# A spiking attention block with a mixture of experts: the last chunk norms from row sums and ScalarE squares, and new orders at both ends

## The reference

```python
def lif_step(v, x_t):              # a leaky neuron: halve the gap, spike at 1, reset
    v = v + (x_t - v) * 0.5
    s = spike(v - 1.0)
    v = v * (1.0 - s)
    return (v, s)

def step(carry, inp):              # scan over the 512 steps
    vr, r = lif_step(vr, r_in); vk, k = lif_step(vk, k_in); vv, v = lif_step(vv, v_in)
    h = h * 0.9 + k * v
    y = r * h

x1 = layernorm(x + y @ Wo.T, ln1_g, ln1_b)          # norm 0
s1 = lif_scan(x1 @ W1.T + b1)
ffn = lif_scan(s1 @ W2.T + b2)
a = layernorm(x1 + ffn, ln2_g, ln2_b)               # norm 1
x3 = _layernorm(x + a)                              # norm 2, the "third" of the title
gates = softmax(x3 @ Wg + bg); keep the best 2 of 8, rescaled
out = _layernorm(x3 + sum over e of gate_e * (x3 @ We_e + be_e))   # norm 3, the "last"
```

## Time and profile before

| | us |
|---|---|
| median of 3 runs | 991.33 (990.92 to 992.54) |
| the profiled execution, its own time | 988.63 |
| its span, first to last instruction | 986.8 |
| PE, DVE busy in the span | 925.7 (94%), 915.6 (93%) |
| ACT, POOL busy in the span | 611.8 (62%), 571.8 (58%) |

### The profile page before, as it was taken

The page is one execution under the profiler, slowest core; times in us unless marked ns, Lnnn a source line. Parts: engine busy times, 40 slices in busy tenths (PEclk is TensorE's granted clock), DMA queues, the critical chain, the costliest instruction groups (busy, mean ns, idle before and its releaser), DMA issues.

```text
span 986.8 us, 20602 instructions
## 1 busy us (share of the span) xinstructions
PE 925.7 (94%) x6506; PEld 859.1 (87%) x6506; DVE 915.6 (93%) x3682; ACT 611.8 (62%) x1389; POOL 571.8 (58%) x731
## 2 busy tenths in 40 slices
PE   5678789999999999999999999999999999999985
PEld 5578688999999999999999999999999999888764
DVE  6489998999999999999999999999999999988975
ACT  4565546666666676666666766667667666556452
POOL 1221113667676666666766666677766666765552
PEclk8799999999999999999999999999999999999999
DMA  8552222555554456555554555655545665456763
GB/s 259 129 108 66 42 54 55 118 119 118 108 112 107 100 122 119 119 122 107 114 107 99 119 118 120 127 111 104 113 97 114 119 127 110 97 97 118 141 127 86
DMA packets 59437, 109.71 MB, mean 111 GB/s; under 512 B 6592, under 2 KB 6592, under 8 KB 59328
## 3 DMA queue, kind: packets, MB, share of 16 engines
q0 software_dynamic: 37728, 68.71, 40.6%
q1 hardware_dynamic: 16992, 31.30, 9.7%
q10 hardware_dynamic: 4608, 8.39, 2.2%
HBM read 31.29 MB, written 8.39 MB: 40 GB/s over the span
## 4 chain that ended last, share of the span: by engine, by line
PE 73%; DVE 15%; ACT 3%; issue 3%; DMA 3%; POOL 2%; SPq 0%; POOLq 0%; ACTq 0%; DVEq 0%
PE ps_e L401 28%; PE ps_proj L401 12%; PE ps_proj L491 10%; PE ps_proj L476 10%; PE ps_proj L497 5%; PE ps_attn L401 3%; DVE U L887 3%; DVE V L894 2%; PE ps_zx L455 2%; DVE stats L966 2%; PE ps_attn L455 1%; DVE h L936 1%; DMA xt<-x_hi 1%; DMA xt<-x_T 1%; DMA acc<-term 1%
## 5 line engine op out<-in xcount | busy, mean ns | idle before, releaser
L887 DVE SCALAR_TENSOR_TENSOR U<-V,U 128x256 f32<-128x256 f32 (+4 forms) x576 | 227.7, 395 | 6.6 <-ACT U L658 2.9
L401 PE MATMUL ps_e<-we_hi,x_hi 128*128 128x512 f32 (+2 forms) x640 | 228.6, 357 | 3.6 <-DVE acc L1109 1.9
L894 DVE SCALAR_TENSOR_TENSOR V<-U 128x256 f32<-128x256 f32 (+4 forms) x576 | 224.2, 389 | 1.6
L401 PE MATMUL ps_e<-we_lo,x_hi 128*128 128x512 f32 (+2 forms) x640 | 223.3, 349 | 0.0
L401 PE MATMUL ps_e<-we_hi,x_lo 128*128 128x512 f32 (+2 forms) x640 | 222.7, 348 | 0.0
L1331 POOL TENSOR_SCALAR s<-U 128x256 fp32r<-128x256 f32 x208 | 192.1, 971 | 16.3 <-DVE V L894 16.3
L1317 POOL TENSOR_SCALAR veps<-mv 128x2 f32<-128x2 f32 x128 | 50.6, 396 | 256.6 <-DVE mv L972 254.4
L697 ACT ACTIVATE term<-ps_e,gate 128x256 f32<-128x256 f32 x372 | 160.3, 475 | 43.3 <-PE ps_e L401 43.3
L658 ACT ACTIVATE U<-ps_proj,cst 128x256 f32<-128x256 f32 x320 | 135.4, 480 | 70.5 <-PE ps_proj L497 64.1
L491 PE MATMUL ps_proj<-x_hi,w_hi 128*128 128x256 f32 x512 | 134.9, 284 | 3.1 <-ACT x_hi L676 1.7
L643 ACT ACTIVATE U<-ps_proj 128x512 f32<-128x512 f32 x96 | 57.6, 600 | 127.2 <-PE ps_proj L401 127.2
(11 more groups left out here) (108 smaller groups left out, 2302.3 us busy)
## 6 DMA issues: line engine op xcount, KB each, us to landing
acc<-term POOLq DMA_DIRECT2D x93, 256.0 KB, 3.7
odd_sum<-term POOLq DMA_DIRECT2D x93, 256.0 KB, 3.3
xt<-x_T SPq DMA_DIRECT2D x33, 256.0 KB, 2.9
xa<-x_tok SPq DMA_DIRECT2D x32, 256.0 KB, 3.2
xt<-x_hi POOLq DMA_DIRECT2D x32, 256.0 KB, 4.3
xb<-cst SPq DMA_DIRECT2D x32, 256.0 KB, 2.3
xb<-x_tok POOLq DMA_DIRECT2D x32, 256.0 KB, 6.1
out<-res ACTq DMA_DIRECT2D x31, 256.0 KB, 2.0
```

What stands on the lines that cost most here:

```text
L401: mm = pe.matmul(dst, lhs, rhs, start=(i == 0), stop=(i == n - 1))
L887: v.scalar_tensor_tensor(out=U[:, s, t, c0:c1], in0=V[:, c0:c1], scalar=0.5, in1=U[:, s, t, c0:c1], op0=ALU.mult, op1=ALU.add).then_inc(do ...
L894: v.scalar_tensor_tensor(out=V[:, c0:c1], in0=u, scalar=THRESHOLD, in1=u, op0=ALU.is_lt, op1=ALU.mult).then_inc(done, 1)
```

## The change

It does the following.

- Norms 2 and 3 no longer use bn_stats and bn_aggr. The VectorE instruction that makes the row also gives its sum (`accum_out`). POOL turns the sums into the negated mean; ScalarE runs two `Square` activations with that mean as bias and accumulates the squares; POOL makes the variance and the power; VectorE multiplies. `res` of norm 3 is made by two instructions of 256 columns instead of one of 512.
- In a steady beat the two squares of norm 2 stand after the first W1 eviction, those of norm 3 after the fourth.
- The x of the second chunk is loaded ahead of the constants and Wo. Its low part is made by VectorE in beat 0, slot 2, not by the POOL DMA and `low_x`.
- TensorE runs 14 further matmuls, whose result nobody reads, after the first R/K/V product (`bridge`).
- In beats 1 to 6 several slots move: norm 0's shift from 8 to 7, the gates, `add_e0`, x1_low (19 in beats 3 and 4, 15 in beat 6), norm 2's shift from 16 to 15, x3_low from 25 to 28. `norm_x3` goes behind the W2 eviction.
- In beats 33 to 38 slots move, the e0 product of the next beat goes ahead of expert step 6, and POOL serves norms 1 and 2 ahead of two of its DMAs.

```diff
-            gate=(4, 5, 6, 7, 8, 12, 13, 14, 15, 16, 24, 26), add_e0=(17, 18),
-            ln1_sum=1, ln1_stats=(2, 3), ln1_aggr=4, ln1_norm=8, x1_low=17,
+            gate=(4, 5, 6, 7, 8, 10, 10, 11, 11, 12, 24, 26), add_e0=(13, 14),
+            ln1_sum=1, ln1_stats=(2, 3), ln1_aggr=4, ln1_norm=7, x1_low=17,
...
-            ln3_stats=10, ln3_aggr=11, ln3_shift=16, x3_low=25,
+            ln3_stats=10, ln3_aggr=11, ln3_shift=15, x3_low=28,
...
+X1_LOW = {3: 19, 4: 19, 6: 15}
+DRAIN = dict(z_sum=-1, y=(-1,) * 5, spikes_h1=-1, fin_sum=11,
...
-             fin_add=17, fin_stats=18, fin_aggr=19, fin_shift=27)
+             fin_add=25, fin_stats=26, fin_aggr=27, fin_shift=31)
+TAIL = dict(DRAIN, add_e0=(5, 5), ln2_scale=(3, 4), x3_low=17)
...
             def beat(b):
-                if b.has(LAG_X):
+                if b.has(LAG_X) and b.k != LAG_X + 1:
                     load_xt(b)
...
                 if b.k == LAG_X:
+                    load_xt(Beat(LAG_X + 1))
                     sp.dma_start(cst[:], consts).then_inc(consts_loaded, 16)
                     sp.dma_start(wo[:], w_o).then_inc(wo_loaded, 16)
...
+            def bridge():
+
+                for _ in range(BRIDGE):
+                    pe.matmul(ps_attn[:, 0, :], wrkv_hi[:, 0, 0:P], wrkv_hi[:, 0, 0:D], start=True, stop=True)
...
+                        if part == 6 and b.late and not b.last_m:
+                            expert0(Beat(b.k + 1))
                         expert(b, part)
                         if part == 4 and b.has(LAG_Z) and b.late:
                             x3_T(b)
-                    if b.late and not b.last_m:
-                        expert0(Beat(b.k + 1))
...
+            def square(ln, src, junk):
+
+                for j in range(TILES):
+                    last = nc.scalar.activation(junk[:, j, :], src[:, j, :], ACT.Square, bias=minus_mean[ln][:, j:j + 1],
+                                                accum_out=squares[ln][:, j:j + 1])
+                last.then_inc(squares_ready[ln], 1)
+
+            def square_x3(b):
+                act.wait_ge(mean_ready[2], b.value(1, LAG_Z, 1))
+
+                if b.has(LAG_Y):
+                    act.wait_ge(x1T_done, b.value(1, LAG_Y, 1))
+                square(2, w, x1n)
+
+            def square_res(b):
+                act.wait_ge(mean_ready[3], b.value(1, LAG_F, 1))
+                square(3, res_of(b), odd_sum[:, b.slot(LAG_F, 2)])
...
                     for f in (0, 1):
                         to_lif(b, fill + f, COL_H1 + 2 * f * B, 2, C_B1 + 2 * f)
+                        if f == 0 and b.has(LAG_Z) and not b.early:
+                            square_x3(b)
...
                     to_lif(b, fill + 3, COL_H1 + 6 * B, 2, C_B1 + 6)
+                if b.has(LAG_F) and not b.late:
+                    square_res(b)
...
                 v.scalar_tensor_tensor(out=w[:, j, :], in0=w[:, j, :], scalar=rstd[1][:, j:j + 1],
-                                       in1=xb[:, j, :], op0=ALU.mult, op1=ALU.add).then_inc(ln2_steps, 1)
+                                       in1=xb[:, j, :], op0=ALU.mult, op1=ALU.add,
+                                       accum_out=sums[2][:, j:j + 1]).then_inc(ln2_steps, 1)
...
-                    v.tensor_tensor(res[:], acc[:, b.slot(LAG_F, 2)], odd_sum[:, b.slot(LAG_F, 2)],
-                                    ALU.add).then_inc(fin_steps, 1)
...
+                    total(odd_sum[:, b.slot(LAG_F, 2)])
...
+            def x_low_second():
+                dve.wait_ge(x_hi_ready, 2)
+                v.scalar_tensor_tensor(out=x_lo[:], in0=xt[:, 1], scalar=-1.0, in1=x_hi[:].bitcast(F32),
+                                       op0=ALU.mult, op1=ALU.subtract).then_inc(x_lo_ready, 1)
...
+            def deviation(b, ln, steps, per, lag, done):
+
+                pool.wait_ge(steps, b.value(per, lag, done))
+                g.tensor_scalar(minus_mean[ln][:], sums[ln][:], -1.0 / D, None, ALU.mult).then_inc(mean_ready[ln], 1)
+                pool.wait_ge(squares_ready[ln], b.value(1, lag, 1))
+                g.tensor_scalar(veps[ln][:], squares[ln][:], 1.0 / D, EPS, ALU.mult, ALU.add).then_inc(rstd_ready[ln], 1)
+                pool.wait_ge(rstd_ready[ln], b.value(2, lag, 1))
+                g.tensor_tensor(rstd[ln][:], veps[ln][:], neg_half[:], ALU.pow).then_inc(rstd_ready[ln], 1)
...
+                if has_z and b.late:
+                    reciprocal_std(b, 1, ln2_steps, LN2_STEPS, LAG_Z, 4)
                 if sums:
                     add_even(b, LAG_F, 6)
```

More of the change, by code:

```diff
@@ L80 @@
 WARM = 5
+BRIDGE = 14
 TERM_SLOTS = E - 2
@@ L246, in build @@
         gate_T = sb("gate_T", [STACK, TILES, P], F32R)
-        stats = [sb(f"stats{i}", [P, TILES, 6]) for i in range(4)]
-        mv = [sb(f"mv{i}", [P, TILES, 2]) for i in range(4)]
+        stats = [sb(f"stats{i}", [P, TILES, 6]) for i in range(2)]
+        mv = [sb(f"mv{i}", [P, TILES, 2]) for i in range(2)]
+        sums, minus_mean, squares = ({i: sb(f"{name}{i}", [P, TILES]) for i in (2, 3)} for name in ("sums", "minus_mean", "squares"))
         veps = [sb(f"veps{i}", [P, TILES]) for i in range(4)]
@@ L285, in build @@
         rstd_ready = [sem(f"rstd_ready{i}") for i in range(4)]
+        mean_ready, squares_ready = ({i: sem(f"{name}{i}") for i in (2, 3)} for name in ("mean_ready", "squares_ready"))
         e0_done, expert_done = sem("e0_done"), sem("expert_done")
@@ L801, in beat @@
                     fill += 1
+                if b.has(LAG_Z) and b.early:
+                    norm_x3(b)
                 if b.has(LAG_Y) and not b.early:
@@ L817, in beat @@
                     read_x3(b)
+                if b.has(LAG_Z) and b.late:
+                    square_x3(b)
                 if b.has(LAG_M) and not b.early and not b.last_m:
@@ L850, in beat @@
                         weight_high(p)
-                if b.has(LAG_X) and b.k > LAG_X:
+                if b.has(LAG_X) and b.k > LAG_X + 1:
                     low_x(b)
@@ L857, in beat @@
                             read_x3(b)
+                        if part == 5 and b.has(LAG_F) and b.late:
+                            square_res(b)
+                if b.has(LAG_F) and (b.last_m or b.k == LAST_BEAT):
+                    square_res(b)
                 if b.has(LAG_F):
@@ L1116, in fin_stage, with total @@
             def fin_stage(b, step):
-                chain = lambda n: after(fin_steps, FIN_STEPS, LAG_F, b, n)
                 if step == 0 and b.k == LAST_BEAT:
                     return
+                def total(other):
+                    for j in range(TILES):
+                        v.scalar_tensor_tensor(out=res_of(b)[:, j, :], in0=acc[:, b.slot(LAG_F, 2), j, :], scalar=1.0,
+                                               in1=other[:, j, :], op0=ALU.mult, op1=ALU.add,
+                                               accum_out=sums[3][:, j:j + 1]).then_inc(fin_steps, 1 + (j == 0 and b.k == LAST_BEAT))
                 if step == 1 and b.k == LAST_BEAT:
@@ L1122, in fin_stage @@
                     dve.wait_ge(term_ready, b.value(E - 1, LAG_F, E - 1))
-                    v.tensor_tensor(res_of(b)[:], acc[:, b.slot(LAG_F, 2)], bias_bank(b.k - 1)[:], ALU.add).then_inc(fin_steps, 2)
+                    total(bias_bank(b.k - 1))
                     return
@@ L1167, in side @@
                 split_w1(b, slot)
+                if b.k == 0 and slot == 2:
+                    x_low_second()
                 if b.k == LAG_Y + 1 and slot == 2 * STEPS - 1:
@@ L1213, in side @@
                             gate_stage(b, step)
-                if b.has(LAG_Y) and slot == at["x1_low"]:
+                if b.has(LAG_Y) and slot == X1_LOW.get(b.k, at["x1_low"]):
                     x1_low(b)
@@ L1227, in side @@
                         ln2_add(b, 1)
-                    if slot == at["ln3_stats"]:
-                        after(ln2_steps, LN2_STEPS, LAG_Z, b, 8)
-                        bn_stats(2, 0, w[:, 0, :], ln3_steps)
-                        bn_stats(2, 1, w[:, 1, :], ln3_steps)
-                    if slot == at["ln3_aggr"]:
-                        bn_aggr(b, 2, ln3_steps, LN3_STEPS, LAG_Z, 2)
                 if b.has(LAG_M):
```

34 lines of the change are left out of this document (16 added, 18 removed).

## The result

The changed kernel takes 1014.01 us, the median of 4 runs (1011.92 to 1014.18), beside 991.31 for the kernel before on the same chip (990.92 to 992.54): a ratio of 1.0222, 95% interval 1.0204 to 1.0240. Forecast were 1009 and a range of 981 to 1023. The profiled execution has a span of 1010.1 us against 986.8, 23.3 more.

The account below looks back on a forecast made before the run. PE bounds the kernel, without a gap in steady beats of 28.06 us. 27.3 (steady) - 7.7 (start and fill) - 1.6 (drain) = +18.0 on 988.63 gives 1006.6; the median lies 2.7 above, so 1009, range 981 to 1023.

Parts of the forecast that it names:

- The steady beats: Beats 7 to 32: two pairs of squares on ACT make PE late, 26 x 1.05 = +27.3 us.
- The stretch on ACT: Steady beat, first W1 eviction to expert step 4's: 7.61 us, 0.96 of it waits; both pairs of squares go there.
- p: Time one pair of squares holds ACT in a steady beat: taken as 1.0 us, by norm 2's pair at 0.99.
- The second ring: Steady beats: squares and POOL make norm 3's shift on DVE 1.5 us later; 0.05 us a beat, 0 to 0.3.
- rival 4: Steady beats: DVE becomes the bound through waits at slots 24 and 29; beat 29.5, time 1018; chance 0.13.
- The start: Second chunk's x loaded earlier: PE's second product at 14.4, third from 27.1 to 29, its end about 5.9 us earlier.
- Beats 3 to 6: Moved slots: beat 3 -0.3, beat 5 +0.4, beat 6 -0.55 and -1.4; together -1.85 us.
- The drain: Last beats: earlier reciprocal and e0 product against slower norms; sum -1.6 us, from -7 to +3.
- reciprocal ahead: Drain, beat 36: POOL's reciprocal of norm 1 ahead of accumulating DMAs is done about 2.3 us earlier, -2.3.
- e0 ahead: Drain: e0 product ahead of step 6 brings the next beat's gates 1.4 us earlier; two beats counted, -2.8.
- longer norm chains: Drain: norms 2 and 3 pass more engines, 0.7 us for each of five norms on the chain, +3.5.
- rival 3: Steady beats: the accumulator read is dear, 1.2 to 1.4 us a pair of squares; time 1024; chance 0.12.

Follow-up runs that it names:

- squares_ahead: Changed kernel with norm 2's scale and add two slots earlier and its squares ahead of the first W1 eviction in steady beats: 1021.88 us, ratio 1.0293.
- edges_only: Changed kernel with norms 2 and 3 by bn_stats and bn_aggr as before, all new orders of start, fill and drain kept: 982.7 us.
- old_drain: edges_only with the whole drain as in the kernel before (slots, POOL's order, e0 product behind expert step 6): ratio 0.9886 to the kernel before.
- pool_only: no_bridge with the changed kernel's drain order on POOL alone, norms by bn_stats: 983.69 us, ratio 0.9916 to the kernel before.
- no_e0_ahead: edges_only with the e0 product of the next beat again behind expert step 6 in the drain: ratio 0.9905 to the kernel before.
- norms_pool: Kernel before with norms 2 and 3 by squares, norm_x3 behind the W2 eviction, and the changed kernel's drain order on POOL alone: 1020.90 us, ratio 1.0286.
- warm_gap: old_drain with 45 more unused matmuls ahead of the first attention product: 979.48 us, ratio 0.987 to the kernel before.
- no_bridge: old_drain without the 14 bridging matmuls ahead of the second product: 979.61 us, ratio 0.9874 to the kernel before.

## Why the prediction was right, and where it was off

**The steady beats: right, step by step.** The stretch on ACT is closed, the pair is 0.98 (I took 1.0), PE waits for `term` before step 6. It waits before step 5 too, which I had not named: 0.27 and 0.74 in the beat shown, and 19.7 / 21 = 0.94 a beat over all. Gates of beat 6 to 32 give +26.0 against +27.3. The beat is 0.96 longer than the one before counted alike (28.10; my 28.06 came from a window that was not 21 whole beats), and I had 1.05. The row that I chose for p, norm 2's pair, was the right one of two: a pair of squares with their sums takes 0.98, that pair 0.99. By the Trainium skill, ScalarE: Activation LUTs, section Rules for kernel authors, the estimate was 1.04 a beat, and the trace agrees to 0.1.

**The second ring.** I put 0.05 on it and made it rival 4 at 0.13. It did not decide, but `squares_ahead` bears out that it was close, 0.17 us a beat by the count of DVE's waits, and waits of 0.89 and 1.74 at the two shifts (forecast about 1 and 1.5) filled it. The sum of rival 4 does not come out: 2.5 us of waits less 0.65 of slack and 1.4 of saved work is 0.45, a beat of 28.5 and not 29.5. Measured, DVE's work fell by 1.1 only, and 26.29 of work and 2.61 of waits are 28.90 of the 29.06. That the ring stayed behind the queue was close, and partly luck.

**The start: right.** PE's second product starts at 13.81 (forecast 14.4), the attention product runs at half clock as bounded, the third product starts at 27.92 (27.1 to 29). Rows of the changed kernel that answer to the earlier trace rows:

```profile
13.81 0.39 PE L407 MATMUL ps_proj<-x_hi,wrkv_hi 128*128 128x256 f32 x1 [0.71 <-DVE x_lo L1204]
```
```profile
24.73 3.75 PE L444 MATMUL ps_attn<-wo,wrkv_raw 128*128 128x256 f32 x8 [6.41 <-DVE wrkv_raw L1002]
27.92 0.78 PE L407 MATMUL ps_proj<-x_hi,wrkv_hi 128*128 128x256 f32 x1
```

**Beats 3 to 6: the sign right, the size too small.** In beat 5, which the earlier trace rows show before, norm 2's shift waits 1.33, not 2.2, and `x3_low` no longer waits. In beat 6 PE's wait for an eviction is gone, and its wait for norm 0 falls from 3.45 to 2.06. What the prediction said of `x1_low` in beat 5 came true: it stands behind the shift, and PE waits 1.60 for it (at 121.14). The slots and the place of `norm_x3` are worth 4.6 us with norms off. What the squares take back in the fill is not shown: `edges_only` and the changed kernel have -11.5 and -10.0 by the gates of beat 6, but `old_drain`, with the same fill code as `edges_only`, has -8.1. That spread is in the profiles, where the granted clock is at 0.50 in other places, and I can't price it.

**The drain: the step that failed.** I had -1.6, as -2.3 (reciprocal ahead), -2.8 (e0 ahead) and +3.5 (longer norm chains); it is +7.3. The chains are near: 7.3 - 4.4 = 2.9 between the changed kernel and `edges_only`, from one profile each. Both gains were not there, though the reciprocal of the earlier trace rows did come ahead and DVE's wait for it fell from 1.25 to 0.38. I had followed the waiting instruction forward to its own consumer and had not asked what stood behind it in the queue that it passed. The e0 product passed step 6, and ACT's `gexp` stood behind step 6. The reciprocal passed a DMA, and the sum of the outputs, in its old slot, stood behind that DMA (`pool_only`). The changed kernel has the sum in a later slot and is spared that wait; but I had not priced the new place of norm 3 at all: its sum now stands behind `x3_low`, and its shift (slot 31) directly ahead of the next `z`. DVE and PE of the changed kernel, beat 34 to 35:

```profile
946.32 0.69 DVE L1063 TENSOR_TENSOR x_lo<-ps_zx,x_hi 128x512 fp32r<-128x512 f32 x1 [1.44 <-ACT x_hi L656]
...
947.25 0.42 DVE L1169 SCALAR_TENSOR_TENSOR res<-acc,odd_sum 128x256 f32<-128x256 f32 x1
...
950.58 0.16 DVE L1021 TENSOR_TENSOR shift<-minus_mean,rstd 128x2 f32<-128x2 f32 x1 [1.31 <-POOL rstd L1365]
950.69 0.76 DVE L954 SCALAR_TENSOR_TENSOR z<-U,x 128x256 f32<-128x256 f32 x2
```
```profile
951.50 0.66 PE L461 MATMUL ps_zx<-cst,z 128*128 128x128 f32 x4 [1.07 <-DVE z L954]
```

3.3 us from the sum to the shift, 1.31 of them waited out, and PE idles 1.07 for `z`. Before, the sum of this beat ran 2.5 us ahead of `x3_low` (927.59 against 930.05) and the shift found its input ready. In `edges_only`, which has the slots without squares, beats 34 to 35 take 17.04 against 15.80; with squares 18.27. `no_e0_ahead` has 17.05, so it is not the e0 order. `norms_pool`, with the old slots and only POOL's order new, loses +4.7 in its drain instead of +7.3, from one profile each.

So of the new orders only POOL's belongs to the squares: in the old slots it gains 13 us with them and loses 4 with `bn_stats`. The new slots and the e0 order lose with `bn_stats` (3.4 by the ratios, POOL's order included), and with squares the drain that has them is 2.6 longer than that of `norms_pool`; by the ratios the gap is no smaller. Which of the two makes it with squares was not run apart. Taken one by one against the kernel before, as I took them, both gains had the wrong sign or none.

**The total, and luck.** The parts missed by -2.3 (start and fill), -1.3 (steady beats) and +8.9 (drain). The first two hide 3.6 of the third, so 1009 against 1014.01 looks better than the account of the drain was. The range is also narrower than the text of the prediction says: it leaves out 1024, the middle of rival 3, and not only its far end.

**What beats both kernels.** `warm_gap` at 979.48 and `no_bridge` at 979.61: the new start and the new fill with `bn_stats` and the old drain, 1.3% faster than before and, by the two ratios to before, 3.4% faster than the changed kernel. They are not separated from each other.

## What to carry to other kernels

Work that moves to an engine with idle time costs what it takes beyond the waits in the one stretch where the bound engine waits for that queue: the first pair fits into 0.96 us of waits, the next ones cost nearly their full length. When a queue's waits are used up, look for the ring that stands next; a move that frees the first can lengthen the second. When an instruction is moved ahead in a queue, price what it passes and who waits for that; one and the same order on POOL was worth -13 us with long chains and +4 with short ones. At the edges, compare medians of runs and not single profiles.
